# Which of several waits an instruction carries, and leaving out waits already made

## The reference, cut to what matters

```python
x = x + 0.5 * ffn(layernorm(x))          # silu(x Wg) * (x Wu), then Wd; 768 hidden
x = x + ssm(layernorm(x))                # selective scan, 16 states, 256 channels
x = x + 0.5 * ffn(layernorm(x))          # same weights
# in ssm: h[t] = a[t] * h[t-1] + b[t] * u[t] per channel and state; y = sum over states of C[t] * h[t]
```

## Time and profile before

| | us |
|---|---|
| median of three runs | 2757.11 (2753.33 to 2761.74) |
| profiled execution | 2749.22 |
| its span, first to last instruction | 2747.4 |
| DVE busy | 2441.3 (89%) |
| POOL busy | 2160.6 (79%) |
| PE busy | 2123.0 (77%) |
| ACT busy | 2022.3 (74%) |
| granted TensorE clock, mean | 0.867 |

### The profile page before, as it was taken

The page is one execution under the profiler, slowest core; times in us unless marked ns, Lnnn a source line. Parts: engine busy times, 40 slices in busy tenths (PEclk is TensorE's granted clock), DMA queues, the critical chain, the costliest instruction groups (busy, mean ns, idle before and its releaser), DMA issues.

```text
span 2747.4 us, 30026 instructions
## 1 busy us (share of the span) xinstructions
PE 2123.0 (77%) x9268; PEld 1156.8 (42%) x9268; DVE 2441.3 (89%) x2548; ACT 2022.3 (74%) x2885; POOL 2160.6 (79%) x1542
## 2 busy tenths in 40 slices
PE   4866688788878878787787878878787877877457
PEld 3433444444444444444444444444444444443234
DVE  3279998999999899999999998999999999999992
ACT  2568687787868778686887878687787868878553
POOL 1368888787878879787897978788798888879672
PEclk9977898888988888898999889898989988888678
DMA  1123333333333333333333333333333333333430
GB/s 60 40 89 134 120 119 108 120 112 130 109 122 124 108 118 116 128 116 115 131 114 117 113 127 114 114 127 106 116 123 131 115 117 130 105 112 116 138 112 19
DMA packets 112290, 308.06 MB, mean 112 GB/s; under 512 B 10913, under 2 KB 45826, under 8 KB 112130
## 3 DMA queue, kind: packets, MB, share of 16 engines
q1 hardware_dynamic: 112130, 306.15, 33.3%
HBM read 288.28 MB, written 17.83 MB: 111 GB/s over the span
## 4 chain that ended last, share of the span: by engine, by line
DVE 29%; PE 22%; issue 21%; POOL 17%; ACT 10%; DVEq 0%; SPq 0%; DMA 0%; POOLq 0%; ACTq 0%
DVE g_bank L960 12%; POOL acc L805 10%; DVE ring L991 10%; PE work L528 7%; PE work L539 5%; PE work L575 4%; DVE hid L919 3%; POOL hid_lo L777 2%; PE work L510 2%; DVE stats L906 2%; ACT ring L741 2%; ACT normed L619 2%; ACT L606 2%; POOL acc L796 1%; POOL rstd L768 1%
## 5 line engine op out<-in xcount | busy, mean ns | idle before, releaser
L805 POOL TENSOR_TENSOR acc<-acc,ring 128x1024 f32<-128x1024 f32 x512 | 1208.6, 2361 | 265.8 <-DVE ring L991 257.3
L960 DVE TENSOR_TENSOR_SCAN g_bank<-du_bank,ring 128x1024 f32<-128x1024 f32 x512 | 1173.4, 2292 | 35.1 <-ACT du_bank L730 4.7
L991 DVE SCALAR_TENSOR_TENSOR ring<-g_bank,inv_a,ring 128x1024 f32<-128x1024 f32 x512 | 653.9, 1277 | 8.5 <-POOL acc L805 1.1
L777 POOL TENSOR_TENSOR hid_lo<-hid,hid_hi 128x512 f16<-128x512 f32 x384 | 447.7, 1168 | 154.2 <-ACT hid_hi L688 153.8
L741 ACT ACTIVATE ring<-dt,a_coef 128x1024 f32<-128x1024 f32 x512 | 546.5, 1137 | 9.9 <-DVE g_bank L960 8.7
L539 PE MATMUL work<-wd_t,hid_hi 128*128 128x256 f16 x1536 | 372.2, 289 | 94.0 <-POOL hid_lo L777 80.2
L528 PE MATMUL work<-xt_hi,wg_t 128*128 128x512 f16 x768 | 323.7, 422 | 136.8 <-DVE hid L919 83.2
L528 PE MATMUL work<-xt_hi,wu_t 128*128 128x512 f16 x768 | 320.6, 417 | 119.0 <-DVE hid L919 66.2
L919 DVE SCALAR_TENSOR_TENSOR hid<-sil,work 128x512 f32<-128x512 f32 x384 | 259.2, 675 | 162.7 <-PE work L528 126.1
L539 PE MATMUL work<-wd_t,hid_lo 128*128 128x256 f16 x1536 | 370.7, 288 | 0.0
L653 ACT ACTIVATE sil<-work 128x512 f32<-128x512 f32 x384 | 219.4, 599 | 190.8 <-DVE hid L919 113.8
(11 more groups left out here) (98 smaller groups left out, 2899.7 us busy)
## 6 DMA issues: line engine op xcount, KB each, us to landing
ring<-c_rows SPq DMA_DIRECT2D x512, 512.0 KB, 3.6
x_in<-L_attn_x SPq DMA_DIRECT2D x32, 512.0 KB, 5.3
out<-x_fin SPq DMA_DIRECT2D x32, 512.0 KB, 5.3
c_rows<-params SPq DMA_DIRECT2D x32, 32.0 KB, 3.1
ring<-L_ffn_w_gate SPq DMA_DIRECT2D x1, 768.0 KB
ring<-L_ffn_w_up SPq DMA_DIRECT2D x1, 768.0 KB
ring<-L_ffn_w_down SPq DMA_DIRECT2D x1, 768.0 KB
ring<-L_attn_W_z SPq DMA_DIRECT2D x1, 256.0 KB
```

The costliest lines, as they stand in the source:

```text
L777: nc.gpsimd.tensor_tensor(hid_lo[:, m, :], hid[:, slot, :], hid_hi[:, m, :], ALU.subtract).then_inc(S["lo"], 1)
L805: nc.gpsimd.tensor_tensor(acc[bt % 2][:, h, :], acc[bt % 2][:, h, :], cg[:, slot, :], ALU.add).then_inc(S["summed"], 1)
L960: scan = nc.vector.tensor_tensor_scan(g_bank[:], du_bank[:], decay[:, a, :], 0.0, ALU.add, ALU.mult)
L991: nc.vector.scalar_tensor_tensor(cg[:, k, :], g_bank[:], inv_a[:, h, s:s + 1], spread[:, k_c, :], ALU.mult, ALU.mult).then_inc(S["weighted ...
```

## The change

A function `hold` keeps, for each engine and semaphore, the highest value that this engine has been made to wait for, and emits a wait only for a higher one. `wait` and `take` go through it. DVE's record is cleared at the start of each of its two programs. Where an event names several waits, their order is changed in six places, so that another one comes first. The operations, their order on each engine, the buffers and the DMAs are the same.

```diff
+        seen = {}
+        def hold(eng, s, n):
+            if seen.get((eng, s), 0) < n:
+                seen[eng, s] = n
+                eng.wait_ge(s, n)
         def wait(eng, what, step, less=0):
-            eng.wait_ge({"ready": ready, "free": free}[what][s] if what in ("ready", "free") else S[s], n - less)
+            hold(eng, {"ready": ready, "free": free}[what][s] if what in ("ready", "free") else S[s], n - less)
...
             def take(job):
-                    pe.wait_ge(free[s], n)
+                    hold(pe, free[s], n)
...
                 if kind == "lx":
+                    wait(act, "rstd", ("lr",) + ev[1:])
                     wait(act, "ready", K.was[ev])
-                    wait(act, "rstd", ("lr",) + ev[1:])
...
                 elif kind == "db":
+                    wait(act, "scanned", ("scan", bt, N - 1, h - 1) if h else ("scan", bt - 1, N - 1, EH - 1))
                     wait(act, "du", ("d", bt, h))
-                    wait(act, "scanned", ("scan", bt, N - 1, h - 1) if h else ("scan", bt - 1, N - 1, EH - 1))
...
                 elif kind == "cm":   # POOL
+                    wait(pool, "weighted", ev)
                     if s == 0:
                         wait(pool, "acc_begun", ("ai", bt, h, NC - 1))
-                    wait(pool, "weighted", ev)
...
             def program(with_tiny):
+                seen.update({key: 0 for key in seen if key[0] is dve})
...
                     elif kind == "sh":
+                        wait(dve, "ready", job)
                         wait(dve, "free", ("ga",) + ev[1:])
-                        wait(dve, "ready", job)
...
                     elif kind == "ra":
+                        wait(dve, "ready", job)
                         wait(dve, f"st{jp // 2}", ("st", bt - 1, jp // 2))
-                        wait(dve, "ready", job)
...
                     elif kind == "scan":
+                        wait(dve, "weighted", earlier(ev, 1))
+                        wait(dve, "decay", ("ex",) + ev[1:])
                         if s == 0:
                             wait(dve, "du_in", ("db", bt, h))
-                        wait(dve, "decay", ("ex",) + ev[1:])
-                        wait(dve, "weighted", earlier(ev, 1))
```

## The result

| | before | after |
|---|---|---|
| median, us (range of 5 runs each, on one chip) | 2757.11 (2753.33 to 2762.34) | 2736.95 (2731.97 to 2738.64) |
| profiled execution, us | 2749.22 | 2737.51 |
| its span, us | 2747.4 | 2735.6 |
| granted TensorE clock, mean | 0.867 | 0.891 |

The ratio of the times is 0.9922 (95% interval 0.9904 to 0.9941): 20.2 us faster. The forecast was 9.6 us, so the sign was right and the time lies inside the range, but the gain is more than double of what the sum gave.

A forecast was written before the change was run, and what follows sets the result against it. The prediction took DVE as busiest, carrying some 45% of a chain with near-equal routes. Its terms, 7.1 + 1.7 + 0.9 - 0.1 = 9.6 us, taken from the median 2757.1 gave 2747.5 us, range 2736 to 2757.

The forecast's parts named there:

- The gap of a pair: DVE scan directly behind the previous slot's product: carrying that wait saves 0.068 us of 0.103 per pair, 19.4 us in all.
- Scans don't begin to wait for decays: On DVE, moving the decay wait into the EVENT_SEMAPHORE costs nothing, since decays are ready early; the contrary would refute the prediction.
- 6.5 of 18 pairs count, 7.1 us: Of each sequence's 18 product-scan pairs on DVE, 6.5 lie on the path: 104 pairs times 0.068 us.
- the five pairs between 1085 and 1141 us: Product-scan pairs in the stretch where the chain stays on DVE, taken as surely on the path; 0.068 us each.
- The longest wait grows by up to 0.7: DVE's longest wait in a period, 4.2 us for a matmul, grows by what the pairs ahead of it save.
- near-equal routes take over: Rival: the route over ACT and PE holds the end, so half the sum, 2 to 6 us, is gained; chance 0.24.
- `sh`, `lx` and the waits left out, 2.5 us: Carried late waits: `sh` for its matmul 1.7 us less 0.1, `lx` for POOL's shift 0.9; waits left out 0.
- slower: `ai` meets POOL: Rival: DVE's second `ai` step falls against long POOL adds more often, 64 times 0.15 to 0.3 us lost; chance 0.05.
- all of DVE's saving counts: Rival: every pair on DVE passes through to the time, about 24 us gained, so 2733; chance 0.2 for 13 to 24.

The follow-up runs named there:

- race-free kernels: Four kernels (before, after, before with only the scan's new wait order, after without it) whose second `ai` step reads the product from PSUM: 2699.55, 2693.43, 2691.76, 2698.40 us.
- order_only: The kernel after with every wait emitted again, so only the six new wait orders are left: 2733.91 us, ratio 0.9918 to the kernel before.
- scan_only_psum: The kernel before with only the scan's waits reordered, and the second `ai` step reading the product from PSUM: 2691.76 us, ratio 0.9774.

## Why the prediction was right in sign and wrong in size

*The gap of a pair.* Right: 103 ns before, 35 after, for all 286. Idle time before scans fell by 19.8 us, forecast 19.4.

*Scans don't begin to wait for decays.* Right: the only named idle before L968 is 5.4 us for `du_bank`, as before.

*6.5 of 18 pairs count, 7.1 us.* The size stands where the race is taken away: the scan's order alone gives 7.8 there, and 5.0 on top of the rest. But the place was wrong. The prediction had the gain in every sequence, in the five pairs between 1085 and 1141 us. The runs show 0.1 us in each of the thirteen middle sequences and 5.7 us in the first and the last two. The agreement in the sum is luck.

*The longest wait grows by up to 0.7.* It went from 4.2 to 4.5 us, as the waits of the stretch from 1101 to 1257 us have it:

```profile
DVE hid L928 <- PE work L536: 5.6, 3, 4.5
```

Half of the forecast. Yet the waits as a whole fell, as the stretch of the thirteen middle sequences has it, before (297.4 to 2389.4 us) and after (298.4 to 2380.7):

```profile
DVE hid L919 <- PE work L528: 68.5, 29, 5.4
DVE hid L919 <- issue: 18.5, 26, 1.0
```
```profile
DVE hid L928 <- PE work L536: 75.7, 51, 4.5
```

From 87.0 to 75.7 us: with the race in the kernel, one wait's length says little. In the race-free kernels the longest wait between 925 and 1082 us stays at 3.9, and a new wait of 1.78 us comes up elsewhere. That is the rival "near-equal routes take over", which the prediction gave 0.24; for the race-free middle sequences it is the right one.

*`sh`, `lx` and the waits left out, 2.5 us.* The order of the waits other than the scan's and `hold` together gave 1.2 us race-free, less than the ranges of those runs (3 to 5 us). The single terms stay unsettled. That the waits left out are worth little agrees with `order_only` against after (3 us apart, in ranges of 5 and 7 us).

*The step that failed* is the price of the rival "slower: `ai` meets POOL". The prediction saw the line with durations from 750 to 2949 ns, named the pair of engines and wrote that "the same mechanism can give as much back", but gave it 0.05, took it over all 64 steps at a mean of 0.15 to 0.3 us, and put only the losing side among the cases. In fact two of the four steps of a sequence run that race, they run it, in the kernel after, at a margin of the size of the gap which the change removes (0.068 us per pair), and a win or a loss moves a whole sequence by 3.5 to 4.6 us. For a change that shifts DVE's timing by that much, this was no rival but a term of the sum, which the forecast left at nothing, with both signs and a range of some 50 us (51 between none won and all won). What the runs show in its place: of the 20.2 us gained, 6.1 remain when the race is taken away, so 14 hang on it. The chance of 0.2 beyond 13 us of gain was put on the wrong mechanism: not "all of DVE's saving counts", whose mark would have been a wait that doesn't grow and a race-free gain of 24.

*What makes up the 11.8 us between the two profiled executions* (spans). The thirteen middle sequences are 9.6 us shorter. In them DVE's gaps of under 0.15 us fell by 16.5 us and its longer waits by 11.1, while the `ai` steps took 19.1 more. By sequence, the one that is won lies 4.5 us below the mean of before, and the other twelve together 5.0, 0.4 each. The first and the last two sequences with head and tail give the other 2.1 (the starts are read to 0.1 us).

*What stays open.* The rest of the 20.2 is 8.4 us between the medians: the profiled execution of before lies under all its timed ones here, by less than the spread of these (9.0 us). That the races fall differently from run to run would give such a spread, and the race-free kernels hardly have one, but no execution without a profile was taken apart. Nor was it settled why the up matmul ahead of the race comes 0.12 us late in one sequence and 0.2 or 1.2 in others.

`scan_only_psum` beats both kernels: 2691.76 us, ratio 0.9774 (0.9758 to 0.9790) to the kernel before, and 45 us below the kernel after. Its gain is the PSUM operand, 54 us, and 7.8 for the scan's wait.

## What to carry to other kernels

Where one line of fixed shape has very different durations, find its opponent in the order of time before predicting anything else: a change that shifts timing by tens of nanoseconds can win or lose the whole of it, many times over. A longer busy time of such a line needn't cost anything: look at the wait ahead of it too. Then take the race out first (one operand from PSUM was enough here), and measure small changes on that version, where their parts add up. The wait that ends last is worth naming first, 0.07 us for each back-to-back pair, but what it brings is decided by which route is the longest at that place, and it may show only at the ends of the kernel.

## What the runs showed of the hardware

- A DVE operation with both tensor inputs in SBUF (128x512, float32) and a POOL add of 128x1024 hold each other up. If DVE wins, its step takes 750 to 753 ns in nearly every case, and the add 2.81 to 2.92 us instead of 2.35. If DVE loses, its step ends 0.55 us behind the add's end, wherever it began: 2.98 us at the longest, 1.85 where it began 1.05 us behind the add. The recorded start doesn't quite decide. In the middle sequences of all kernels DVE lost with a head start of up to 50 ns and won from 56 ns on; in the sequence bt = 14 it lost with 66 and 78 ns in two kernels, and won with 82 in another. With one of the two inputs in PSUM the step takes 746 to 750 ns always, beside the same adds, and no add takes over 2.39 us.
- The price of a wait depends on who makes it. A DVE instruction that carries the wait on its own predecessor starts 35 ns behind its end, and 103 ns if the wait is in an EVENT_SEMAPHORE. Between engines, counted from the semaphore's update in the two traces: 23 against 80 ns on DVE (`sh` behind its matmul), 22 against 83 on ACT (`db` behind the scan), 44 against 135 on PE (L589 before, behind ACT's L710).
- An added POOL operation of 0.20 us in each sequence made a kernel of 2737 us faster by 19.7 us.
